# Preparing the convolution kernel of a fused S4D and gated FFN kernel: complex product regrouped, five products on GpSimd, shorter TensorE filler, 384 and 128 columns at the end

## What is computed

```python
dt = jnp.exp(log_dt)
A = -jnp.exp(log_A_real) + 1j * A_imag
dtA = A * dt[:, None]
Ct = Cc * (jnp.exp(dtA) - 1.0) / A
P = dtA[:, :, None] * jnp.arange(length)
K = 2.0 * jnp.einsum('hn,hnl->hl', Ct, jnp.exp(P)).real
y = causal_conv(x, K) + x * D[:, None]      # then masked by length
hidden = silu(fq(y) @ gate.T) * (fq(y) @ up.T)
out = x + fq(hidden) @ down.T               # fq rounds to fp8 and back
```

## Time and profile before

| | us |
|---|---|
| median of three runs (lowest, highest) | 325.48 (325.44, 325.55) |
| the profiled execution's own time | 325.52 |
| its span, first to last instruction | 323.8 |
| TensorE busy | 310.2 (96%) |
| VectorE busy | 303.2 (94%) |
| ScalarE busy | 206.9 (64%) |
| GpSimd busy | 12.5 (4%) |
| mean granted TensorE clock | 1.000 |

### The profile page before, as it was taken

One profiled execution on the slowest core, in us unless ns is written; L12 is line 12 of the kernel. 1 busy time (PEld: TensorE's weight loads), 2 busy tenths in 40 slices (PEclk: granted clock), 3 DMA queues, 4 the chain that ended last, 5 costly groups with the idle time before them and its releaser, 6 DMA issues.

```text
span 323.8 us, 4771 instructions
## 1 busy us (share of the span) xinstructions
PE 310.2 (96%) x1569; PEld 162.9 (50%) x1595; DVE 303.2 (94%) x464; ACT 206.9 (64%) x318; POOL 12.5 (4%) x20
## 2 busy tenths in 40 slices
PE   1999999999999999999999999999999999989996
PEld 1467554545455554555455454555455454534444
DVE  6999999999999999999998999989998999989784
ACT  4858788188755777486845868376863959364540
POOL 2031000000001000010001000010001000010010
PEclk9999999999999999999999999999999999999999
DMA  6879999300002690078202780067401650051028
GB/s 201 181 181 231 268 278 383 148 1 2 0 0 28 150 343 3 1 130 279 110 0 36 165 317 1 0 121 249 150 0 16 134 243 0 0 97 34 2 31 228
DMA packets 14014, 38.38 MB, mean 119 GB/s; under 512 B 1470, under 2 KB 6558, under 8 KB 11052
## 3 DMA queue, kind: packets, MB, share of 16 engines
q1 hardware_dynamic: 8412, 26.58, 23.2%
q0 software_dynamic: 5584, 11.57, 20.6%
HBM read 33.90 MB, written 15.81 MB: 154 GB/s over the span
## 4 chain that ended last, share of the span: by engine, by line
PE 72%; DVE 19%; issue 4%; ACT 4%; DMA 1%; DVEq 0%; ACTq 0%
PE gate_ps L547 19%; PE up_ps L547 18%; PE down_ps L503 17%; PE y_ps L489 15%; DVE hv L860 3%; DVE yq L844 3%; DVE yt L833 2%; DVE hq L877 2%; DVE ht L868 2%; PE y_ps L598 1%; DVE ym L825 1%; PE down_ps L598 1%; ACT hc L381 1%; DMA prm<-in_params 1%; DVE hq L885 1%
## 5 line engine op out<-in xcount | busy, mean ns | idle before, releaser
L398 ACT ACTIVATE sil<-gate_ps,fac 128x512 f32<-128x512 f32 (+1 forms) x88 | 59.6, 680 | 67.8 <-PE gate_ps L547 66.8
L547 PE MATMUL gate_ps<-yq,wg 128*128 128x512 bf16 (+3 forms) x365 | 88.2, 363 | 2.7 <-DVE hv L860 2.4
L547 PE MATMUL up_ps<-yq,wu 128*128 128x512 bf16 (+3 forms) x367 | 88.4, 363 | 0.3
L489 PE MATMUL y_ps<-xt,toep 128*128 128x512 f32 (+1 forms) x248 | 78.1, 434 | 0.0
L503 PE MATMUL down_ps<-wd,hq 128*128 128x512 bf16 (+1 forms) x295 | 76.8, 379 | 0.7
L860 DVE SCALAR_TENSOR_TENSOR hv<-up_ps,fac,sil 128x512 f32<-128x512 f32 (+1 forms) x88 | 65.5, 744 | 8.2 <-ACT sil L398 6.6
L381 ACT ACTIVATE hc<-hv 128x1024 f32<-128x1024 f32 (+1 forms) x48 | 47.0, 980 | 20.9 <-DVE hq L877 19.8
L547 PEld LDWEIGHTS gate_ps<-yq,wg 128*128 128x128 bf16 x372 | 35.6, 100 | 43.6 <-ACT sil L398 4.0
L489 PEld LDWEIGHTS y_ps<-xt,toep 128*128 128x128 f32 x248 | 45.9, 190 | 19.9 <-issue 2.4
L868 DVE SCALAR_TENSOR_TENSOR ht<-hc,hv 128x1024 f32<-128x1024 f32 (+1 forms) x48 | 54.1, 1127 | 1.9 <-ACT hc L381 1.9
L547 PEld LDWEIGHTS up_ps<-yq,wu 128*128 128x128 bf16 x372 | 36.3, 100 | 38.3
(11 more groups left out here) (155 smaller groups left out, 118.1 us busy)
## 6 DMA issues: line engine op xcount, KB each, us to landing
xt<-in_xT SPq DMA_DIRECT2D x8, 1024.0 KB, 7.6
out<-in_x SPq DMA_DIRECT2D x7, 1024.0 KB, 5.6
out<-res POOLq DMA_DIRECT2D x7, 1024.0 KB, 7.8
toep<-kpad_scratch SPq DMA_DIRECT2D x6, 1024.0 KB, 10.0
toep<-kpad_scratch SPq DMA_DIRECT2D x8, 256.0 KB, 3.9
wd<-in_down POOLq DMA_DIRECT2D x1, 1280.0 KB, 21.3
xt<-in_x SPq DMA_DIRECT2D x1, 1024.0 KB, 7.3
out<-xt SPq DMA_DIRECT2D x3, 256.0 KB, 3.1
```

What stands on the lines that cost most here:

```text
L398: nc.scalar.activation(sil[b][0:w, :], gate_ps[b][0:w, :], ACT.Silu, scale=fac[0:w, S_GATE:S_GATE + 1]).then_inc(silu_done, 1)
L489: last = nc.tensor.matmul(y_ps[h % 2][:, d * P:L], toep[par][:, h, d * P:(d + 1) * P], xt[par][:, h, 0:L - d * P], start=(d == 0), stop=(d ...
L547: mm = nc.tensor.matmul(ps[b][0:w, cols], wt[:, k, c * P:c * P + w], yq[par][:, version, k, cols], start=(k == 0), stop=(k == LB - 1))
```

## The change

- The gain. Let Q = exp(i angle) - 1 (real part `cos1`, imaginary part the sine) and let h be 2 C over A, which the code before calls g. Before, (E + 1) Q + E is formed first and then multiplied by g. Now h Q is formed first (`h_cos`, `h_sin`, `turned`), and the result is (E + 1) (h Q) + E h. E's last Horner step is multiplied by two to the k through `rt_x` in the same instruction.
- GpSimd computes five products and sums of 16 or 32 columns (|A|^2 and the numerator of h) after its first two weight loads' issue and a wait for `decay_ready`; VectorE waits for `norm_ready` and `gain_ready`.
- D of group 0 goes ahead of its taps: a 64-column matmul of a row that holds D and zeros (`dsk_first`, loaded with `unit`, whose rows grow from 128 to 192 floats) opens the sum, and the last tap matmul of each half signals `k_ready`.
- WARM is (0, 2, 4): no small filler ahead of the taps of group 0, two small ones behind, then four of 512 columns.
- |turns| of groups 1 and 2 is a VectorE instruction (`magnitude_of_turns`) with a semaphore `whole_ready`; ScalarE keeps group 0. The length masks move: two go ahead of the last subtraction of group 2's phase, two behind `g_of(1)`.
- t = 3 of the end is split 384 and 128 columns (3 * P) instead of 256 and 256, in the matmuls and in LAST_PARTS.

The diff, with the declarations of semaphores, the `unit` load of SP (now the whole `unit_tile`) and LAST_PARTS left out:

```diff
@@ -48,7 +48,7 @@
 K_GROUPS = [slice(0, FIRST), slice(FIRST, 6), slice(6, JC)]
-WARM = (2, 14)
+WARM = (0, 2, 4)
 EARLY, MIDDLE = 2 * P, 5 * P
@@ -141,8 +141,11 @@
         dec = inside(hq[0], 0, JC, M)
-        one_by_one, by_step = inside(hq[0], JC * M, 1, P), inside(hq[0], JC * M + P, LATE, M)[0:LATE]
-        decay_t = inside(hq[0], JC * M + P + LATE * M, 1, P)[0:LATE]
+        unit_tile = inside(hq[0], JC * M, 1, P + FIRST * KB)
+        one_by_one = unit_tile[:, :, 0:P]
+        dsk_first = unit_tile[:, 0, P:].rearrange("p (j b) -> p j b", b=KB)
+        by_step = inside(hq[0], JC * M + P + FIRST * KB, LATE, M)[0:LATE]
+        decay_t = inside(hq[0], JC * M + P + FIRST * KB + LATE * M, 1, P)[0:LATE]
         gu, gv = inside(hq[1], 0, JC, 2, KA), inside(hq[1], 2 * JC * KA, JC, 2, KA)
@@ -287,6 +292,18 @@
             pool.dma_start(wu[:, :, 0:EARLY], wu_d[:, :, 0:EARLY]).then_inc(up_in, 16)
+            def s(i, n=1):
+                return sm[:, i:i + n, :]
+            pool.wait_ge(decay_ready, 1)
+            nc.gpsimd.tensor_tensor(s(27), s(9), s(9), ALU.mult).then_inc(gain_chain, 1)
+            nc.gpsimd.tensor_tensor(s(31, 2), s(37, 2), s(9).broadcast_to([P, 2, JC]), ALU.mult).then_inc(gain_chain, 1)
+            pool.wait_ge(gain_chain, 1)
+            nc.gpsimd.tensor_tensor(s(27), s(27), s(28), ALU.add).then_inc(norm_ready, 1)
+            pool.wait_ge(gain_chain, 2)
+            nc.gpsimd.tensor_tensor(s(33), s(31), s(30), ALU.subtract)
+            nc.gpsimd.tensor_tensor(s(34), s(29), s(32), ALU.add).then_inc(gain_ready, 1)
             pool.wait_ge(toep_first[HB - 1], 16)
@@ -331,9 +348,13 @@
                 act.wait_ge(turns_ready, i + 1)
-                nc.scalar.activation(whole[:, js], turns[:, js], ACT.Abs).then_inc(abs_turns_ready, 1)
+                if i == 0:
+                    nc.scalar.activation(whole[:, js], turns[:, js], ACT.Abs).then_inc(abs_turns_ready, 1)
                 nc.scalar.activation(wave[:, js, 1], turns[:, js], ACT.Sin, scale=-TURN)
-                act.wait_ge(abs_turns_ready, i + 1)
+                if i == 0:
+                    act.wait_ge(abs_turns_ready, 1)
+                else:
+                    act.wait_ge(whole_ready, i)
                 nc.scalar.activation(wave[:, js, 0], whole[:, js], ACT.Sin, bias=cst[:, M:M + 1],
@@ -440,6 +461,18 @@
+            def unit_terms(i):
+                js = K_GROUPS[i]
+                for half in range(2):
+                    row = slice(N * half, N * half + 1)
+                    unit_row = cst[row, UNIT:UNIT + KA]
+                    if i == 0:
+                        nc.tensor.matmul(k_in_bank(0, half), unit_row, dsk_first[row], start=True, stop=False)
+                    else:
+                        nc.tensor.matmul(k_in_bank(i, half)[:, :, 0], unit_row, dsk[row, js],
+                                         start=False, stop=True).then_inc(k_ready, 1)
             def k_of(i):
@@ -447,12 +480,18 @@
                         for half, rows in enumerate(halves):
-                            nc.tensor.matmul(k_in_bank(i, half)[:, j - js.start], gk[rows, j, t],
-                                             wave[rows, j, t, 0:KB], start=(j == js.start and t == 0), stop=False)
-                for half in range(2):
-                    row = slice(N * half, N * half + 1)
-                    nc.tensor.matmul(k_in_bank(i, half)[:, :, 0], cst[row, UNIT:UNIT + KA], dsk[row, js],
-                                     start=False, stop=True).then_inc(k_ready, 1)
+                            last = i == 0 and j == js.stop - 1 and t == 1
+                            mm = nc.tensor.matmul(k_in_bank(i, half)[:, j - js.start], gk[rows, j, t],
+                                                  wave[rows, j, t, 0:KB], start=(i > 0 and j == js.start and t == 0),
+                                                  stop=last)
+                            if last:
+                                mm.then_inc(k_ready, 1)
+                if i:
+                    unit_terms(i)
+            def warm_small(count):
+                for n in range(count):
+                    nc.tensor.matmul(y_ps[n % 2][:, 0:6 * JC + CONSTS], prm[:, 0:P], prm[:], start=True, stop=True)
@@ -467,11 +506,12 @@
                                  stop=True).then_inc(dec_arg_ready, 1)
-            for n in range(WARM[0]):
-                nc.tensor.matmul(y_ps[n % 2][:, 0:6 * JC + CONSTS], prm[:, 0:P], prm[:], start=True, stop=True)
+            unit_terms(0)
+            warm_small(WARM[0])
             k_of(0)
+            warm_small(WARM[1])
             pe.wait_ge(gate_in, 16)
-            warm(WARM[1])
+            warm(WARM[2])
             k_of(1)
@@ -587,8 +627,8 @@
                                     (2, range(6), full), (0, range(8, CH), full), (1, range(8, CH), full),
-                                    (2, range(6, CH), full), (3, range(CH), slice(0, L // 2)),
-                                    (3, range(CH), slice(L // 2, L))):
+                                    (2, range(6, CH), full), (3, range(CH), slice(0, 3 * P)),
+                                    (3, range(CH), slice(3 * P, L))):
                 for k in chunks:
@@ -634,23 +674,23 @@
             thetas, kt, r = s(15, 3), s(0, 3), s(10, 3)
-            x, kx, rx, qx, two_x = s(19), s(20), s(21), s(22), s(23)
-            expm1, norm, half = s(25), s(27), s(28)
-            c_ai, c_ar, g = s(29, 2), s(31, 2), s(33, 2)
-            gre, gim = s(33), s(34)
-            sr, si, g_sr, g_si = s(35), s(36), s(29, 2), s(31, 2)
+            x, kx, rx, qx, two_x, rt_x = s(19), s(20), s(21), s(22), s(23), s(24)
+            expm1, norm, ai2 = s(25), s(27), s(28)
+            c_ai, c2, h = s(29, 2), s(37, 2), s(33, 2)
+            h_cos, h_sin, turned, cos1 = s(29, 2), s(31, 2), s(35, 2), s(26)
             def both(ap):
                 return ap.broadcast_to([P, 2, JC])
             ex, ek, er, eq, two_k = pr[:, 0:2, :], s(0, 2), s(2, 2), s(4, 2), s(6, 2)
             e = did(v.tensor_scalar(ex, ex, -87.0, 88.0, ALU.max, ALU.min))
-            v.tensor_tensor(c_ai, cc, both(ai), ALU.mult)
+            v.tensor_scalar(c2, cc, -2.0, None, ALU.mult)
             after(e)
             e = did(v.tensor_scalar(ek, ex, LOG2E, MAGIC, ALU.mult, ALU.add))
-            v.scalar_tensor_tensor(half, ai, 0.5, ai, ALU.mult, ALU.mult)
+            v.tensor_tensor(ai2, ai, ai, ALU.mult)
             after(e)
             e = did(v.tensor_scalar(ek, ek, MAGIC, None, ALU.subtract))
+            v.tensor_tensor(c_ai, c2, both(ai), ALU.mult)
             after(e)
@@ -739,41 +779,39 @@
             b = did(v.scalar_tensor_tensor(qx, qx, 1.0 / math.factorial(5), rx, ALU.add, ALU.mult))
-            c = did(v.scalar_tensor_tensor(norm, ar, 0.5, ar, ALU.mult, ALU.mult))
+            v.tensor_scalar(two_x.bitcast(I32), kx, 127.0, 2.0 ** 23, ALU.add, ALU.mult)
+            dve.wait_ge(norm_ready, 1)
+            c = did(v.reciprocal(norm, norm))
             after(b)
             b = did(v.scalar_tensor_tensor(qx, qx, 1.0 / math.factorial(4), rx, ALU.add, ALU.mult))
-            v.tensor_tensor(c_ar, cc, both(ar), ALU.mult)
             after(b)
             b = did(v.scalar_tensor_tensor(qx, qx, 1.0 / math.factorial(3), rx, ALU.add, ALU.mult))
-            c = did(v.tensor_tensor(norm, norm, half, ALU.add))
+            v.tensor_tensor(rt_x, rx, two_x, ALU.mult)
+            dve.wait_ge(gain_ready, 1)
+            after(c)
+            c = did(v.tensor_tensor(h, h, both(norm), ALU.mult))
             after(b)
             b = did(v.scalar_tensor_tensor(qx, qx, 1.0 / math.factorial(2), rx, ALU.add, ALU.mult))
-            v.tensor_scalar(two_x.bitcast(I32), kx, 127.0, 2.0 ** 23, ALU.add, ALU.mult)
-            after(b)
-            b = did(v.scalar_tensor_tensor(qx, qx, 1.0, rx, ALU.add, ALU.mult))
-            c = did(v.reciprocal(norm, norm))
-            after(b)
-            b = did(v.tensor_tensor(qx, qx, two_x, ALU.mult))
-            v.tensor_tensor(gre, s(30), s(31), ALU.subtract)
-            c = did(v.tensor_tensor(gim, s(29), s(32), ALU.add))
+            dve.wait_ge(sines_ready, 1)
+            a = did(v.scalar_tensor_tensor(cos1, s(SIN_HALF), -2.0, s(SIN_HALF), ALU.mult, ALU.mult))
+            after(b)
+            b = did(v.scalar_tensor_tensor(qx, qx, 1.0, rt_x, ALU.add, ALU.mult))
             after(c)
+            c = did(v.tensor_tensor(h_sin, h, both(s(SIN)), ALU.mult))
+            after(a)
+            a = did(v.tensor_tensor(h_cos, h, both(cos1), ALU.mult))
+            after(b)
             b = did(v.scalar_tensor_tensor(expm1, two_x, -1.0, qx, ALU.add, ALU.add))
-            dve.wait_ge(sines_ready, 1)
-            a = did(v.scalar_tensor_tensor(sr, s(SIN_HALF), -2.0, s(SIN_HALF), ALU.mult, ALU.mult))
-            c = did(v.tensor_tensor(g, g, both(norm), ALU.mult))
             after(a)
-            a = did(v.scalar_tensor_tensor(sr, expm1, 1.0, sr, ALU.add, ALU.mult))
```

(56 more changed lines are left out.)

## The result

The change makes the kernel slower, and above all uneven.

| | median | lowest | highest |
|---|---|---|---|
| before | 325.56 | 325.39 | 326.06 |
| after | 327.13 | 325.46 | 328.23 |

What follows compares the result with a forecast made beforehand. VectorE's queue was taken to bound the first 20 us, the steady state being untouched. Sooner product and taps were given back by its queue: 325.52 + 0.18 = 325.70 us, range 325.0 to 326.9.

Steps and rivals of the forecast that it cites:

- part 5: First results: TensorE 0.05 to 0.1 us sooner, second half of `ym` at 20.15; all of +0.18 us reaches the steady state.
- Part 1: Gain product on VectorE, from the Horner step at 8.09 to line 788: 0.47 us sooner, at 10.50 instead of 10.97.
- Part 2: GpSimd's five products and sums: 0 on the path, still covered at an upper bound of 0.51 us each.
- Rival 2: GpSimd holds up VectorE's small steps from 6.0 to 7.5 us, up to 0.85 us later, 326.5; chance 8%.
- Part 3: Taps of group 0: VectorE's copies start at 11.89, 0.61 us sooner, store and Toeplitz reads with them; reads have little to give.
- Parts 4 and 5: VectorE's queue behind the copies, through to the first results: line 957 is 0.18 us later, all of it reaching the steady state.
- Part 6: The end, t = 3 split 384 and 128: last step 0.13 us shorter, larger store late; 0, bounds -0.25 and +0.25.
- rival 1: TensorE's clock still low at `k_of(1)`: 326.6 us, up to 327, 16%; never raised by float32, some 330, 4%.

Runs made afterwards that it cites:

- a_fill10: The changed kernel with ten wide filler matmuls in place of four: 325.68 us, ratio 1.0006 to the kernel before.
- b_fill4: The kernel before with four wide filler matmuls in place of fourteen, nothing else: 327.20 us, ratio 1.0052.
- a_late4: The changed kernel with its four wide filler matmuls held back until VectorE has group 2's phase ready: 326.56 us, ratio 1.0024.
- ones_abs: The changed kernel with magnitudes of groups 1 and 2 on ScalarE, three and ten wide fillers on a tile of ones around group 0's taps: 325.13 us.
- a_early: The changed kernel with sixteen more wide filler matmuls on a tile of ones, ahead of its own four: 327.10 us, ratio 1.0062.
- best: The changed kernel with early filler, eighteen wide fillers on a tile of ones behind the taps, magnitudes of groups 1 and 2 on ScalarE: 325.41 us.

## Why the prediction was wrong, step by step

The forecast was 325.7 us in a range of 325.0 to 326.9; measured were 327.13. The sum of VectorE's queue held; the term of TensorE, put at "0.05 to 0.1 sooner" in part 5, and the choice between cases failed.

- **Part 1, the product.** -0.47 us predicted for the stretch from the Horner step to the gain product. It is 2.35 (8.17 to 10.52) instead of 2.88: -0.53. From `decay` on it is 0.30 shorter in the profiled execution and 0.50 in a_fill10, the difference being what GpSimd takes back. That the gain product started at 10.52, for the 10.50 predicted, is partly luck: VectorE reached `decay` 0.15 sooner (5.69 for 5.84), and GpSimd cost 0.20.
- **Part 2, GpSimd.** 0 on the path, each up to 0.51: the instructions are 0.21 to 0.29 long and finish by 7.28, a microsecond before they are wanted. Rival 2 is there too in this one execution, at 0.20 us instead of up to 0.85.
- **Part 3, the taps.** Copies at 11.89 predicted, 11.91 measured. That the reads have little to give was right, but they don't come the full 0.61 sooner: the first lands at 17.28 instead of 17.73, since the store ahead of them takes 1.75 us to land instead of 1.41.
- **Parts 4 and 5, VectorE's queue.** Line 957 at 19.75 predicted, 19.77 measured (19.74 in a_fill10); the two-input price of the magnitudes was the right one, 0.34 and 0.66 long. +0.18 on the steady state predicted, +0.10 measured with the filler restored.
- **Part 5, TensorE.** The second half of `ym` was to come at 20.15; it came at 21.43, behind a convolution that ended at 21.40. With the filler restored (a_fill10) it came at 20.08.
- **Part 6, the end.** 0 predicted; 0.1 gained by the traces, within the bounds given.
- **The step that failed is this full-speed TensorE of part 5, and with it the chance given to rival 1**, 16% for its first form. The prediction saw the filler go from fourteen wide matmuls to four, and even priced the case: a convolution end near 21.6 and 326.6 us; the profiled execution has 21.40 and 326.61. It then held against it that "float32 work may count in part, and any rise by 16.9 is in time". The rise wasn't in time: `k_of(1)` took 1.04 us in the profiled executions of the changed kernel, b_fill4 and a_late4. By their times the low clock is the rule: eight of ten runs are above 326.0, b_fill4 is above 326.6 in all six, and with float32 filler alone one run of six was fast. What was at hand and underweighted: in the trace of before no rise had come out of the float32 work from 7.09 on, and 2.9 us of wide matmuls had run before it did, against 1.7 us left. And those 2.9 us, from one execution, were taken as a fixed amount, where with one and the same filler the rise came 1.2 us behind the first wide matmul in one execution and 2.8 in another.
- **The price of rival 1 was one value of many.** Runs reach 328.23, 2.8 above the fastest. How long the low level lasts differs between executions, up to nearly the whole of TensorE's first two groups of convolution matmuls as in b_fill4's profiled one (327.27). No run above 327.3 was profiled, so what the runs near 328 lose beyond that isn't shown. The range took the single price for the upper end. The Trainium skill (TensorE: Matmul & The Clock Gate, Part 1) says that the moment of the rise isn't tied to the kernel's start and so varies between runs; the traces agree: 14.21 and 15.82 for the same filler.

The rival that the idleness behind the short filler lowers a raised clock has little left: 1.33 us (ones_abs) and 1.23 us (a_early) didn't, where the changed kernel has 1.54. Not settled: the step from 1.33 to 1.54 us, and why in the profiled execution of the `best` version a raised clock was low again by 9.1 us, behind float32 work on 14 rows and idle stretches of no more than 1 us.

## What to carry to other kernels

Filler matmuls are part of the timing even when nobody reads them: before cutting them, see in several traces what had run when the level rose, since one trace shows one value of many, and take the cut as a risk once less than the largest is left. Let the filler end ahead of the first matmul that matters even at the low level: 1.33 us of idleness behind it did no harm here, 3.2 us did, and filler that ran on held the work up. Judge such a change by ten runs, not by one profile, since its cost shows as spread. And when one engine's queue is shortened, look at once at what stands beside the chain: here the Toeplitz reads, which in a_fill10 landed at 17.30 for matmuls that started at 17.54.
